# Layer 0 of a graph network: the gates' product per tile in quarters of PE's columns, and one transpose for the gates instead of two

## What is computed

```python
row, col = (edge_index[0], edge_index[1])
e = jnp.concatenate([x[row], x[col]], axis=-1)
g1 = _lrelu(jnp.einsum('ef,hgf->heg', e, gate_w1))
alpha = _lrelu(jnp.einsum('heg,hog->heo', g1, gate_w2))
w_edge = pos[col][None, :, None]
a = w_edge * jnp.exp(alpha)
seg = lambda t: jax.ops.segment_sum(t, row, num_segments=N_NODES)
rowsum = jax.vmap(seg)(a)
inv = 1.0 / rowsum + 1e-16
alpha_n = a * inv[:, row]
m1 = _lrelu(jnp.einsum('ef,hgf->heg', e, msg_w1))
beta = _lrelu(jnp.einsum('heg,hog->heo', m1, msg_w2))
out_h = jax.vmap(seg)(alpha_n * beta)
return jnp.mean(out_h, axis=0)
```

## Time and profile before

| | |
|---|---|
| time, median of 3 runs | 6826.49 us (6826.26 to 6827.18) |
| span of the profiled execution | 5851.6 us |
| time less span | 974.9 us |
| PE busy | 4355.2 us (74%) |
| DVE busy | 4656.5 us (80%) |
| POOL busy | 3496.4 us (60%) |
| ACT busy | 2612.7 us (45%) |
| transfers | 437.02 MB, mean 75 GB/s |

### The profile page before, as it was taken

The page is one execution under the profiler, slowest core; times in us unless marked ns, Lnnn a source line. Parts: engine busy times, 40 slices in busy tenths (PEclk is TensorE's granted clock), DMA queues, the critical chain, the costliest instruction groups (busy, mean ns, idle before and its releaser), DMA issues.

```text
span 5851.6 us, 116285 instructions
## 1 busy us (share of the span) xinstructions
PE 4355.2 (74%) x25010; PEld 2801.2 (48%) x25010; DVE 4656.5 (80%) x10137; ACT 2612.7 (45%) x6383; POOL 3496.4 (60%) x3689
## 2 busy tenths in 40 slices
PE   6214999999999999999999999545555555455455
PEld 4212555555555555555555555334444444444444
DVE  9887988989889898988989889756666666666665
ACT  5102777777777777777777777510000000000000
POOL 1002656666565665656656566367777777777776
PEclk9656999999999999999999999855555555555555
DMA  6601333333333333333333333333333323322332
GB/s 247 130 0 47 78 79 80 77 80 79 78 81 78 78 80 78 81 78 78 81 78 80 79 78 80 97 73 59 56 56 56 59 56 56 60 56 56 60 56 51
DMA packets 459109, 437.02 MB, mean 75 GB/s; under 512 B 268369, under 2 KB 340274, under 8 KB 457906
## 3 DMA queue, kind: packets, MB, share of 16 engines
q0 software_dynamic: 122512, 173.81, 18.0%
q1 hardware_dynamic: 308706, 249.41, 15.3%
q10 hardware_dynamic: 27840, 13.23, 1.4%
HBM read 363.27 MB, written 72.83 MB: 75 GB/s over the span
## 4 chain that ended last, share of the span: by engine, by line
PE 46%; POOL 17%; issue 13%; DVE 12%; DMA 6%; ACT 4%; ACTq 1%; SPq 0%; POOLq 0%; DVEq 0%
PE ps_hidden L1814 9%; POOL work L853 9%; PE ps_beta L1866 9%; POOL ends L853 8%; PE ps_hidden L1815 7%; PE ps_beta L1874 7%; DMA ends<-src_table,src_quads 5%; PE ps_alpha L1848 4%; DVE work L1429 4%; DVE work L1317 4%; PE ps_sum L1885 3%; ACT beta_scaled L949 3%; PE ps_T L1803 3%; PE ps_alpha L1857 2%; DVE work L1739 1%
## 5 line engine op out<-in xcount | busy, mean ns | idle before, releaser
L751 POOL DMA_INDIRECT ends<-split_table,src_pairs x1612 | 1581.0, 981 | 1571.7 <-issue 1435.0
L1317 DVE TENSOR_TENSOR work<-work,ps_hidden 128x512 f32<-128x512 f32 x1612 | 1102.3, 684 | 25.4 <-ACT work L897 6.5
L1814 PE MATMUL ps_hidden<-ends_parts,w_high 128*128 128x512 f32 x2418 | 1064.4, 440 | 60.5 <-DVE work L1317 58.8
L897 ACT ACTIVATE work<-ps_hidden 128x512 f32<-128x512 f32 x1612 | 960.6, 603 | 63.2 <-PE ps_hidden L1815 34.6
L1815 PE MATMUL ps_hidden<-ends_hot,window 128*128 128x512 f32 x2418 | 953.4, 394 | 0.0
L853 POOL DMA_INDIRECT work<-src_table,src_quads x808 | 764.4, 946 | 309.2 <-issue 222.0
L853 POOL DMA_INDIRECT ends<-src_table,src_quads x804 | 760.5, 946 | 245.2 <-issue 226.0
L2038 PE MATMUL ps_beta<-work,dst_rows_sb 128*128 128x128 f32 x1608 | 416.4, 441 | 565.6 <-DVE work L1745 565.6
L1115 ACT ACTIVATE ps_alpha<-dots 128x8 f32<-128x8 f32 x403 | 72.7, 180 | 1676.4 <-DVE dots L1707 1676.4
L1866 PE MATMUL ps_beta<-work,msg_w_sb 128*64 128x512 f32 x3224 | 804.1, 609 | 0.4 <-DVE work L1317 0.2
L2038 PE MATMUL ps_beta<-work,equal 128*128 128x128 f32 x1616 | 417.2, 440 | 509.1 <-DVE work L1745 509.1
(11 more groups left out here) (204 smaller groups left out, 6650.2 us busy)
## 6 DMA issues: line engine op xcount, KB each, us to landing
window<-window_table SPq DMA_DIRECT2D x403, 192.5 KB
parts<-in_edge_attr SPq DMA_DIRECT2D x101, 512.0 KB
dst_rows_sb<-by_src SPq DMA_DIRECT2D x403, 128.0 KB
ends<-split_table,src_pairs POOLq DMA_INDIRECT x1612
window_table<-parts SPq DMA_DIRECT2D x49, 386.0 KB, 2.4
sums<-key_rows POOLq DMA_DIRECT2D x403, 32.6 KB
work<-src_table,src_quads POOLq DMA_INDIRECT x808, 2.5
ends<-src_table,src_quads POOLq DMA_INDIRECT x804, 2.5
```

The lines of the kernel that those rows point to most:

```text
L751: pool.indirect_dma_start(out=ends[m][:, t, :], out_offset=None, in_=split_table, in_offset=bass.IndirectOffsetOnAxis(ap=src_pairs[m // 2] ...
L897: nc.scalar.activation(scaled[k % NL][:, :], ps_hidden[k % NL][:, :], ACT.Copy, scale=SLOPE).then_inc(scaled_ready, 1)
L1317: nc.vector.tensor_tensor(hidden[k][:, :], scaled[k % NL][:, :], ps_hidden[k % NL][:, :], ALU.max).then_inc(hidden_ready, 1)
L1814: nc.tensor.matmul(o, w1_high[:, k * P:(k + 1) * P], ends_parts[j][:, :], start=True, stop=False)
```

## The change

`gate_product` now runs eight matmuls of 128 columns instead of four of 256. Each of the four tiles has a quarter of the array's columns; chunk 0 starts the sum in PSUM, chunk 1 adds to it. The two heads of chunk 1 therefore lie in columns 2 and 3 of its weights, so that a tile's 32 rows begin with its four gates. The result is 128x128: `copy_gates` copies 128 columns instead of 256, and `turn_gates` needs one transpose instead of two. The 16 numbers per partition are then read at four places of four instead of eight places of two.

```diff
-        gates_T = parts_flat[1][:, ZW + NB * T + T * W0:ZW + NB * T + T * W0 + 2 * P]
+        gates_T = parts_flat[1][:, ZW + NB * T + T * W0:ZW + NB * T + T * W0 + P]
...
-        alpha_turned = ps_alpha[:, 2 * P:4 * P].rearrange("p (t c r) -> p t c r", c=2, r=WIN0)[:, :, :, 0:2]
+        alpha_turned = ps_alpha[:, 2 * P:3 * P].rearrange("p (t r) -> p t r", r=WIN0)[:, :, 0:H]
...
-                sp.dma_start(gate_w2_sb[(h % 2) * D:(h % 2 + 1) * D, h // 2, h % 2:h % 2 + 1],
+                sp.dma_start(gate_w2_sb[(h % 2) * D:(h % 2 + 1) * D, h // 2, h:h + 1],
...
-                nc.scalar.activation(gates_T, ps_alpha[:, 0:2 * P], ACT.Copy).then_inc(gates_copied, 1)
+                nc.scalar.activation(gates_T, ps_alpha[:, 0:P], ACT.Copy).then_inc(gates_copied, 1)
...
-                for f in range(2):
-                    for c in range(2):
-                        at = (2 * f + c) * WIN0
-                        last = nc.tensor.matmul(ps_alpha[at:at + WIN0, 0:2 * P], gate_w2_sb[:, c, :],
-                                                hidden[c].rearrange("p (i f e) -> p i f e", f=2, e=P)[:, :, f, :],
-                                                start=True, stop=True)
+                for c in range(2):
+                    for t in range(T):
+                        last = nc.tensor.matmul(ps_alpha[t * WIN0:(t + 1) * WIN0, 0:P], gate_w2_sb[:, c, :],
+                                                hidden[c][:, t * P:(t + 1) * P], start=(c == 0), stop=(c == 1))
                 last.then_inc(gates_done, 1)
...
-                for i in range(2):
-                    last = nc.tensor.transpose(ps_alpha[:, (2 + i) * P:(3 + i) * P], gates_T[:, i * P:(i + 1) * P],
-                                               ident[:, :])
-                last.then_inc(gates_turned, 1)
+                nc.tensor.transpose(ps_alpha[:, 2 * P:3 * P], gates_T, ident[:, :]).then_inc(gates_turned, 1)
```

More of the change, by code:

```diff
@@ L965, in scale_alpha @@
                 wait(act, alpha_ready, b)
-                nc.scalar.activation(alpha_scaled[:, :].rearrange("p (t c r) -> p t c r", c=2, r=2), alpha_turned, ACT.Copy,
+                nc.scalar.activation(alpha_scaled[:, :].rearrange("p (t h) -> p t h", h=H), alpha_turned, ACT.Copy,
                                      scale=SLOPE).then_inc(alpha_scaled_ready, 1)
@@ L1374, in edges0_windows @@
                 wait(dve, exp_ready, b)
-                nc.vector.tensor_tensor(alpha[:, :].rearrange("p (t c r) -> p t c r", c=2, r=2),
-                                        alpha_scaled[:, :].rearrange("p (t c r) -> p t c r", c=2, r=2), alpha_turned,
+                nc.vector.tensor_tensor(alpha[:, :].rearrange("p (t h) -> p t h", h=H),
+                                        alpha_scaled[:, :].rearrange("p (t h) -> p t h", h=H), alpha_turned,
                                         ALU.max).then_inc(alpha_ready, 1)
@@ L1825, in second_product @@
                     if k < 2:
-                        o, w = ps_alpha[:, t * H + 2 * k:t * H + 2 * k + 2], gate_w2_sb[:, k, 0:2]
+                        o, w = ps_alpha[:, t * H + 2 * k:t * H + 2 * k + 2], gate_w2_sb[:, k, 2 * k:2 * k + 2]
                     else:
```

## The result

The changed kernel takes 6760.4 us (median of 4 runs, 6753.82 to 6762.84) against 6826.84 for the kernel before: ratio 0.99, 95% interval 0.9886 to 0.9914, 66 us faster. The forecast was 6785.4 with a range of 6779 to 6810. The sign was right; the time lies outside the range, on the quick side.

A forecast was written before the change was run, and what follows sets the result against it. PE's work was taken to be in layer 0's chain of each block; -0.11 us (transpose) + 0.008 (product) = -0.102 per block, times 403 = -41.1, giving 6785.4 us from 6826.49, range 6779 to 6810.

The forecast's parts named there:

- What bounds layer 0: Layer 0 loop: PE's work is in the chain of each block, so its edited steps count once per block, 403 times.
- The removed transpose, -0.11: `turn_gates` on PE: one of two transposes, charged 0.22 together, goes, saving 0.11 us per block.
- The product, +0.008: `gate_product` on PE: 16 passes in four groups, same 512 columns, two more group starts, +0.008 us per block.
- The upper end: `gate_product`: three later groups each pay 0.022 for half-hidden loads, +0.066, net -0.044 us per block, 6809 us; chance 0.07.
- the rival that feeds a pass in no less than 55 ns: `gate_product`: passes cannot be fed faster, product takes 0.88 us instead of 0.46, +0.31 per block, 6951 us; chance 0.07.
- The 0.11 behind the last group: Gap from the product's last group to the next transpose: might shrink a little with shorter passes, allowed -0.008 us.
- The quad's sum: PE step of the same four-quarter form, 261 columns, groups every 0.222 us: used to get 0.002 us per group beyond columns.
- the transposes' row: PE's 128x128 turns follow each other every 0.11 us though their loads last 140 ns: argued against the upper end.
- ACT's copy, worth nothing: `copy_gates` on ACT: 0.276 instead of 0.385 us per block, no gain because ACT then waits 0.63 us for PE.
- Room for 0.1 us: DVE, next to be late, idles 0.40 us before `rectify_pair`, 0.69 per block in the mean, so a 0.1 gain fits.
- The sum: Whole kernel: -0.11 + 0.008 = -0.102 us per block, times 403 is -41.1 us, expected 6785.4 us; chance 0.80.
- the 974.9 between them: Difference of profiled span 5851.6 and timed median 6826.49 us, taken to hold no kernel instruction and kept unchanged.

The follow-up runs named there:

- section 3: Kernel before, two turns and wide copy timed on one slower chip: 6837.72, 6843.85 and 6776.88 us.
- two turns: Changed kernel with a second gates' transpose put back into columns nobody reads: 5845.21 us on a quick chip, 6843.85 on a slower one.
- wide copy: Changed kernel with ACT writing its 128 columns twice, so the copy is as long as before: 5800.24 us quick chip, 6776.88 slower.

## Why the prediction was right in its terms and missed the time

**What bounds layer 0: right on the quick kind.** PE's list is the chain, and an edit to it counts once per block. A transpose put back costs 0.110 us per block on the quick chip. On the kind that was timed the edit does not count alike in every block, and behind the change PE's list sets the pace in one block of four only (section 3).

**The removed transpose, -0.11: right on the quick kind.** The chain charges 0.11 instead of 0.22. On the kind that was timed it is more, as said under the sum.

**The product, +0.008: right, and a little high.** It came to +0.002 per block by the times (-0.010 to +0.016), and to +0.005 by the starts of its passes. The upper end (+0.066, loads half hidden) and the rival that feeds a pass in no less than 55 ns do not occur: 16 passes take the 0.57 us of the 8. The 0.11 behind the last group did not shrink either. The quad's sum was the right row to size a group by; that the loads' records are as long as a group of 128 columns streams did not matter, as the transposes' row had said. The Trainium skill ("TensorE: Matmul & The Clock Gate", section "Wait — 56ns, not 53.3ns?") gives about 62 ns per matmul for a sequencer with hardware decode off. No such bound is met here: 16 passes in 0.57 us are 36 ns each, 32 in 0.58 are 18, and counted as the program's 16 matmuls of two passes 36. Whether hardware decode is off in these runs no trace tells.

**ACT's copy, worth nothing: right** on the kind of chip that the forecast's trace came from (-44.1 with the long copy, -43.7 with the short one). On the slower kind the gain is 61 us with the long copy and 64.5 and 66 with the short one, on different chips, which is no difference clear of the noise.

**Room for 0.1 us: right** on the quick kind. DVE keeps 0.28 us of idle time where it had 0.40, and takes over only about 0.3 us further on.

**The sum: this step failed.** It read "the 974.9 between them lie outside the recorded span and hold no instruction of the kernel, so I keep them". They were not outside. The trace and the timed runs were of two kinds of chip: the timed ones spend the 975 us inside, in waits, as the spans of 6761.0 and 6836.8 us show; about 200 of them lie in layer 0, in the very loop that the change edits. On the quick kind the forecast of -41.1 meets -43.7; on the kind that was timed the same edit brings -64.5 and -66.0. The terms had been priced by a trace in which every step is seen at once by who waits for it, and applied to runs in which it is not. Of the sum, the term for the transpose was mis-sized there: it was put at -0.11 us per block, and the second transpose put back costs 0.17 (two turns 67 us over the wide copy on one chip; 67 / 403), the whole change bringing -0.16 (66 / 403) instead of -0.102. A path was missing too: on these chips the second block of each turn runs over an ACT that sees a chunk late, and the change shortens that by half a microsecond. The range had no such case, because the 975 us were explained away where they were the one number that did not fit.

**What stays open.** What holds the finished steps back on those chips, and why the hold-up falls on chunk 3 with the second transpose in place and on chunk 4 without it. The traces show that it moves, that two turns bring it back on the same chip and that a message's transpose moves it in fewer turns; no run shows what decides it. So the part of the gain beyond 0.11 us per block is located, not explained.

None of the kernels here that do the whole of the reference's work is faster than the changed one.

## What to carry to other kernels

Set the span of the profiled execution beside the timed median before anything is priced: here they differed by about 2 us whenever trace and time were of the same run. Where they differ by more, the trace is of another condition than the times, and a sum made from it needs a range for that. A matmul narrow enough for a quarter of the array can be cut along its columns into twice as many pieces for almost nothing (0.005 us here, at 128 columns), and that is worth doing if the layout that comes out saves a transpose on the engine whose list is the chain. The copy that became shorter here brought nothing.

## What the runs showed of the hardware

- The same kernel took 5844 and 5845 us on two chips and 6766, 6827, 6831 and 6838 on others, each steady within 0.3%. The instructions are as long (DVE 329 and 330 ns in the mean over layer 1); the waits are longer. No chip was measured twice.
- On the slower ones ACT started 1.45 us after the matmuls it waited for had ended (0.04 elsewhere), while PE went on, and did so at the same place in every turn of the loop (median 1.43).
- Four quarters of the array take their passes as a group at the columns' rate down to 64 columns: from the first pass to the next transpose 8 passes of 256 columns take 0.570 us, 16 of 128 take 0.575, 32 of 64 take 0.585. Cut so fine, half of the products took 0.73 and 0.77 on the slower chips.
- Behind the last group of a product the next 128x128 transpose starts about 0.115 us later than its columns alone would give, with 256, 128 and 64 columns alike (0.330, 0.223 and 0.170 us from start to start, of which 0.216, 0.108 and 0.054 are columns at 0.842 ns).
